# Sender attribute sums of a graph kernel: one-hots of 448 as the moving operand, attributes in two 12-bit parts

## The reference

```python
def _scatter_mean(vals, idx, num_segments):
    s = segment_sum(vals, idx, num_segments)
    cnt = segment_sum(ones(len(vals)), idx, num_segments)
    return s / maximum(cnt, 1.0)[:, None]
rec_attr  = _scatter_mean(edge_attr, row, N)     # row = src: the sender
sent_attr = _scatter_mean(edge_attr, col, N)     # col = dst: the receiver
out = concatenate([x, rec_attr, sent_attr], axis=1)
h = out @ W1 + b1;  h = where(h >= 0, h, 0.01 * h);  x + (h @ W2 + b2)
```

## Time and profile before

| what | value |
|---|---|
| median of 3 runs | 2954.69 us (2952.81 to 2959.83) |
| profiled execution | 2959.81 us, its span 2958.0 us |
| TensorE (PE) busy | 1953.7 us, 66% of the span |
| VectorE (DVE) busy | 1936.3 us, 65% |
| GpSimd (POOL) busy | 912.5 us, 31% |
| ScalarE (ACT) busy | 548.4 us, 19% |
| L1312, five matmuls of 425 columns x 83 | 312.7 us busy |
| L1328, 75 x 25 block matmuls | 293.9 + 147.7 us busy |
| L874, the products | 319.0 us busy |

### The profile page before, as it was taken

One profiled execution on the slowest core, in us unless ns is written; L12 is line 12 of the kernel. 1 busy time (PEld: TensorE's weight loads), 2 busy tenths in 40 slices (PEclk: granted clock), 3 DMA queues, 4 the chain that ended last, 5 costly groups with the idle time before them and its releaser, 6 DMA issues.

```text
span 2958.0 us, 37499 instructions
## 1 busy us (share of the span) xinstructions
PE 1953.7 (66%) x10211; PEld 1468.2 (50%) x10211; DVE 1936.3 (65%) x4804; ACT 548.4 (19%) x1179; POOL 912.5 (31%) x886
## 2 busy tenths in 40 slices
PE   3666679999999998535244334288745655656657
PEld 2211148877788886324233223277734444444446
DVE  8777777769877777646355436875575555556555
ACT  2444420000000001100000000022223333333332
POOL 2000000000000000276676677220025556556550
PEclk9666679999999999765555555588856667677778
DMA  5223244423443441334343343244211111111110
GB/s 172 116 123 133 113 156 175 171 82 129 156 178 106 172 173 63 113 103 114 103 131 105 107 114 106 68 117 125 85 41 41 41 40 43 42 43 43 40 42 27
DMA packets 98715, 299.72 MB, mean 101 GB/s; under 512 B 21472, under 2 KB 48871, under 8 KB 86240
## 3 DMA queue, kind: packets, MB, share of 16 engines
q1 hardware_dynamic: 69566, 232.90, 22.8%
q0 software_dynamic: 27712, 63.56, 8.2%
q10 hardware_dynamic: 1250, 0.86, 0.1%
HBM read 220.27 MB, written 76.97 MB: 100 GB/s over the span
## 4 chain that ended last, share of the span: by engine, by line
PE 41%; DVE 19%; POOL 14%; issue 13%; another core or an unknown queue 10%; DVEq 2%; ACT 1%; DMA 1%; ACTq 0%; SPq 0%; POOLq 0%
PE PS L1328 13%; PE PS L1312 8%; POOL G L520 8%; PE PS L1467 6%; PE PS L1432 5%; POOL SCR L520 5%; DVE SCR L848 3%; PE PS L1302 3%; DVE RX L1167 2%; DVE G L847 2%; DVE SCR L874 2%; PE PS L1455 2%; DVEq L1167 1%; DVE OH L836 1%
## 5 line engine op out<-in xcount | busy, mean ns | idle before, releaser
L520 POOL DMA_INDIRECT G<-table,src_idx x255 | 270.6, 1061 | 1271.8 <-DMA table<-RX 1164.4
L537 POOL DMA_INDIRECT G<-table,gather_idx x415 | 417.2, 1005 | 527.1 <-DMA table<-RX 247.6
L1387 PE MATMUL PS<-RX,OH 128*128 x830 | 224.0, 437 | 317.5 <-issue 247.8
L1167 DVE TENSOR_TENSOR RX<-RX,PS 128x256 f32 x415 | 173.0, 417 | 293.5 <-remote 241.1
L1387 PEld LDWEIGHTS PS<-RX,OH 128*128 128x128 f32 x830 | 185.6, 313 | 358.5 <-issue 356.3
L1467 PE MATMUL PS<-SCR,OH 128*128 128x256 f32 x830 | 281.0, 502 | 94.3 <-DVE SCR L1202 73.0
L874 DVE TENSOR_TENSOR SCR<-G,AT 128x2125 f32<-128x2125 f32 x83 | 319.0, 3843 | 0.0
L1312 PE MATMUL PS<-SCR,OH 128*128 128x425 f32 x830 | 312.7, 523 | 2.2 <-DVE G L882 1.8
L1328 PE MATMUL PS<-HB,RX 128*128 128x132 f32 (+1 forms) x2500 | 293.9, 278 | 1.0 <-ACT RX L590 1.0
L1302 PE MATMUL PS<-SCR,G 128*128 128x400 bf16 x590 | 212.4, 487 | 115.6 <-DVE SCR L848 53.0
L1328 PEld LDWEIGHTS PS<-HB,RX 128*128 128x128 f32 x2500 | 285.3, 192 | 1.5 <-ACT RX L590 1.5
(11 more groups left out here) (298 smaller groups left out, 2595.1 us busy)
## 6 DMA issues: line engine op xcount, KB each, us to landing
RX<-adjacency SPq DMA_DIRECT2D x66, 1600.0 KB, 6.7
adjacency<-RX SPq DMA_DIRECT2D x25, 1600.0 KB, 5.2
RX<-gathered_rows SPq DMA_DIRECT2D x83, 320.0 KB, 2.9
gathered_rows<-G SPq DMA_DIRECT2D x51, 320.0 KB
AT<-dst_in_block SPq DMA_DIRECT2D x83, 160.0 KB
gathered_rows<-SCR SPq DMA_DIRECT2D x32, 320.0 KB
G<-table,gather_idx POOLq DMA_INDIRECT x415
G<-table,src_idx POOLq DMA_INDIRECT x255
```

What stands on the lines that cost most here:

```text
L520: pool.indirect_dma_start(score_rows(i)[:, q], None, tables[0], bass.IndirectOffsetOnAxis(ap=src_idx[:, v:v + 1], axis=0)).then_inc(s(f"sc ...
L537: pool.indirect_dma_start(G[:, p, q, :], None, tables[i], bass.IndirectOffsetOnAxis(ap=gather_idx[:, p, q:q + 1], axis=0)).then_inc(s(f"{n ...
L1167: dve.tensor_tensor(acc, acc, PS[:, q, 0:MSG], ALU.add).then_inc(s("added"), 1)
L1387: ins = pe.matmul(view(PS, k % DEPTH * 1024 + 171 * q, [[1, XR_W]]), view(OH, (k % DEPTH * VB + q) * P, [[1, P]]), view(RX, b * XR_W, [[1, ...
```

## The change

The senders' sum is turned around. The 3125 nodes are cut into 7 groups of 448. The stationary operand holds 7 x 17 = 119 columns, the attributes times "is this the sender's group", and the moving one is a one-hot of 448, the sender's place in its group. Both are `float32r`, a second fp32 type of the tensor engine. The attributes are cut into two parts, the upper 20 bits of the word (sign, exponent, the leading bits of the mantissa) and the rest, so there are two matmuls for each visit, ten for each batch. The sums now lie as 119 rows (group, attribute) by 448 nodes, so the counts must be spread over 16 rows by one matmul and the means picked out by seven others. The batches lie in steps 0 to 62 (20 of these have two), and the means are made among steps 63 to 72 and not behind step 74.

```diff
+FULL = 63
+GRP = 7
+NSRC = 448
+LA = GRP * SA
+PARTS_L = 2
-            BATCH_OF.append([k, k + 1] if NBLK <= n < NBLK + NB - LAYERS * NBLK else [k])
+        BATCH_OF = [list(range(NB * n // FULL, NB * (n + 1) // FULL)) if n < FULL else [] for n in range(LAYERS * NBLK)]
 def attr_batch(k):                                            # VectorE
                 dve.tensor_copy(part(0), attrs(16))
-                split = mark(dve.tensor_tensor(sbh([[NBLK, VB], [1, NBLK]]), ..., ALU.is_equal))
-                one_hot(OHS(p), 2, k)
+                is_in()
+                split = mark(dve.tensor_scalar(half(HIGH_AT).bitcast(I32), attrs(SA).bitcast(I32), 12, 12, ALU.logical_shift_right,
+                                               ALU.logical_shift_left))
+                for q in range(VB):
+                    dve.tensor_scalar(hot_src(p, q), iota_h[:, 0:NSRC], view(EI, 2 * VW + VB * k + q, [[1, 1]]), None, ALU.is_equal)
                 dve.wait_ge(s("dve_step"), split)
-                dve.tensor_tensor(products(p), sbh([[NBLK, VB], [1, NBLK], [0, SA]]),
-                                  view(AT, VB * k, [[1, VB], [0, NBLK], [NV + 1, SA]]), ALU.mult)
+                dve.tensor_tensor(left, attrs(16), part(0), ALU.subtract)
+                split = mark(dve.tensor_tensor(half(LOW_AT), attrs(SA), half(HIGH_AT), ALU.subtract))
+                dve.tensor_tensor(into(0), member, by_group(HIGH_AT), ALU.mult)
                 dve.wait_ge(s("dve_step"), split)
                 split = mark(dve.tensor_copy(part(1), left))
+                dve.tensor_tensor(into(1), member, by_group(LOW_AT), ALU.mult)
+                dve.wait_ge(s("dve_step"), split)
+                split = mark(dve.tensor_tensor(left, left, part(1), ALU.subtract))
...
 def attr_sums(k):                                             # TensorE
                 for q in range(VB):
-                    pe.matmul(PS[:, 2, 0:NBLK * SA], OHS(p)[:, q], products(p)[:, q], start=False, stop=False, skip_group_check=True)
+                    for j in range(PARTS_L):
+                        pe.matmul(PS[0:LA, 2, 0:NSRC], grouped(p, j)[:, q * LA:(q + 1) * LA], hot_src(p, q),
+                                  start=False, stop=False, skip_group_check=True)
...
 VectorE, after update_block(n):
+                if n == FULL:
+                    attr_means()
+                if n == FULL + 2:
+                    dve.wait_ge(s("src_means_picked"), 1)
+                    src_sums = view(SUMS, 0, [[1, NSRC]], LA)
+                    dve.tensor_tensor(src_sums, src_sums, PS[0:LA, 2, 0:NSRC], ALU.mult).then_inc(s("means_ready"), 1)
...
 TensorE, after the batches of step n:
+                if n == FULL + 1:
+                    pe.wait_ge(s("means_ready"), 1)
+                    pe.matmul(PS[0:LA, 2, 0:NSRC], view(SUMS, 2 * NSRC, [[1, LA]], LA), view(SUMS, NSRC, [[1, NSRC]], LA), ...)
+                    pe.wait_ge(s("means_ready"), 2)
+                for g in range(7):
+                    if n == FULL + 1 + (g + 1) // 2:
+                        turn_means(g)
+                    if n == FULL + 6 + (g + 1) // 2:
+                        pick_means(g)
 setup, for each of four groups of visits:
-                dve.tensor_scalar(view(HT, 1536, [[1, P]]).bitcast(I32), idr[:, 0:P], 7, None, ALU.arith_shift_right)
-                dve.tensor_scalar(view(HT, 1664, [[1, P]]).bitcast(I32), idr[:, 0:P], 127, None, ALU.bitwise_and)
+                dve.tensor_scalar(sixteenth, idr[:, 0:P], 4, None, ALU.arith_shift_right)
-                dve.tensor_copy(st[2], view(HT, 1664, [[1, P]]).bitcast(I32))
-                dve.tensor_copy(vc, view(HT, 1536, [[1, P]]).bitcast(I32))
+                dve.tensor_scalar(group, sixteenth, 73.0, 36.0, ALU.mult, ALU.add)
+                dve.tensor_scalar(sixteenth, group, 11, None, ALU.arith_shift_right)
+                done(dve.tensor_copy(vc, sixteenth))
+                dve.tensor_scalar(st[2], vc, -float(NSRC), 1.0, ALU.mult, ALU.add)
+                dve.tensor_tensor(st[2], st[2], st[0], ALU.add)
```

More of the change, by code:

```diff
@@ L72 @@
 assert CB * CHUNKS == NBLK
+assert GRP * NSRC >= NODES and all((s * 73 + 36) >> 11 == s * SUBW // NSRC for s in range(SUBS))
 assert NB * VB == NV and (NB - PEEL) % DEPTH == 0 and 24 <= SLOT and AB * AV == NVA and SUBS % 2 == 0
@@ L104, in gnn_program @@
         HT = (RX, HT_AT)
+        with nc.sbuf_tensor("HOT_R", [P, 2 * VB * NSRC], F32R) as HOT_R:
+            pass
         SCR = sb("SCR", [P, 7680])
@@ L107, in gnn_program @@
         EI = sb("EI", [P, 5, VW])
+        with nc.sbuf_tensor("GROUPED_GAP", [P, DEPTH * VB * (D + P) - 4 * VB * LA - 4], F32):
+            with nc.sbuf_tensor("GROUPED_R", [P, 4 * VB * LA], F32R) as GROUPED_R:
+                pass
         G = sb("G", [P, DEPTH, VB, D])
@@ L119, in gnn_program @@
         iota = sb("iota", [P, P])
-        iota_h = sb("iota_h", [P, KEYS + P], mybir.dt.int16)
+        iota_h = sb("iota_h", [P, NSRC + P], mybir.dt.int16)
         zeros_b = sb("zeros_b", [P, KEYS], BF16)
@@ L867, in attr_batch @@
-                sbh = lambda dims: view(G, SBH_AT + p * VB * NBLK, dims)
+                left = view(G, LEFT_AT, [[16, VB], [1, 16]])
+                half = lambda at: view(G, at, [[SA, VB], [1, SA]])
+                by_group = lambda at: view(G, at, [[SA, VB], [0, GRP], [1, SA]])
+                into = lambda j: grouped(p, j).rearrange("p (v g a) -> p v g a", v=VB, g=GRP)
                 dve.tensor_copy(part(0), attrs(16))
-                split = mark(dve.tensor_tensor(sbh([[NBLK, VB], [1, NBLK]]), view(iota, 0, [[0, VB], [1, NBLK]]),
-                                               view(EI, VW + VB * k, [[1, VB], [0, NBLK]]), ALU.is_equal))
@@ L871, in attr_batch @@
-                one_hot(OHS(p), 2, k)
+                is_in()
[3 more added lines that the diff above has]
+                    dve.tensor_scalar(hot_src(p, q), iota_h[:, 0:NSRC], view(EI, 2 * VW + VB * k + q, [[1, 1]]), None, ALU.is_equal)
                 dve.wait_ge(s("dve_step"), split)
-                split = mark(dve.tensor_tensor(left, attrs(16), part(0), ALU.subtract))
@@ L1317, in attr_sums, with turn_means, pick_means @@
                 ins.then_inc(s("attrs_summed"), 1)
+            def turn_means(g):
+                w = min(4, NBLK - 4 * g)
+                if g >= 2:
+                    pe.wait_ge(s("mt_ready"), g - 1)
+                for b in range(w):
+                    ins = pe.transpose(PS[0:32, 4 + g % 2, b * P:(b + 1) * P], means[:, 4 * g + b, :], ident[:])
+                ins.then_inc(s("means_turned"), 1)
+            def pick_means(g):
+                if g == 0:
+                    pe.wait_ge(s("means_ready"), 3)
+                if g >= 2:
+                    pe.wait_ge(s("mt_ready"), 7 + g - 1)
+                pe.matmul(PS[0:16, 6 + g % 2, 0:NSRC], ident[0:LA, g * SA:g * SA + 16], view(SUMS, 0, [[1, NSRC]], LA),
+                          start=True, stop=True).then_inc(s("src_means_picked"), 1)
             pe.wait_ge(s("pair_copied"), SUBS // 2)
```

88 lines of the change are left out of this document (48 added, 40 removed).

## The result

The changed kernel takes 2857.8 us (median of 4 runs, 2853.9 to 2861.7) against 2957.3 us of the kernel before on the same chip (2952.8 to 2965.3): a ratio of 0.966 (95% interval 0.963 to 0.969), faster by 99 us. The forecast was 2832 us, with a range of 2800 to 2900. The profiled execution took 2858.4 us, its span 2856.6.

What follows compares the result with a forecast made beforehand. TensorE was taken to set the time of the 75 steps. Terms of -138 + 7.7 - 1 - 2.8 + 1.5 + 8.2 + 1.9 gave -122.5 us: 2837 from the profiled execution, 2832 from the median, range 2800 to 2900.

Steps and rivals of the forecast that it cites:

- TensorE's batches: Attribute matmuls of the 83 batches: 3.69 us a batch becomes 2.03, at one pass a matmul; 306 becomes 168 us, -138.
- stalls at steps 25 and 50: TensorE's waits at layer changes, 6.8 and 5.9 us, plus 4.4 for slow steps: 17.1 against 9.4 before, +7.7 us.
- start: Beginning of the 75 steps: batch 0 comes 1.2 us earlier, a gain of 1 us.
- eight doubles of before: The eight steps with two batches in the kernel before, bound by VectorE: -2.8 us.
- VectorE late in the first layer: Before the first layer change, where VectorE's margin is thin, a little lateness: +1.5 us.
- tail: Means moved among steps 64 to 72: 11.3 us more on TensorE, less 3.1 gained at the norm, +8.2 us.
- setup: VectorE's extra operations per group of 128 visits, +0.46 us for each of four groups: +1.9 us.
- the rivals of two and four passes: Attribute matmuls take two passes (2985 us, chance 0.03) or four (3298 us, chance 0.05), slower than before.
- The rival of loads that aren't hidden: Weight loads of the attribute matmuls stand open: +94 us, at most 2926 us; chance 0.06.
- limit of the first layer: VectorE's batch stays hidden up to 5.44 us in the first layer; forecast batch 5.26, 0.18 to spare.
- sign "near 1036": Sign in the trace: the norm behind the 75 steps begins near 1036 us instead of 1161.
- That the clock might fall: Clock falling in the shorter gaps, among other things 1 to 3% late; chance 0.05.

Runs made afterwards that it cites:

- true_fp32: The changed kernel with both operands of the attribute matmuls in plain fp32, all else the same: 3063.0 us, ratio 1.125 to the kernel before.
- columns: The changed kernel with 448, 352, 256 or 192 moving columns in the attribute matmuls, by batch in turn: 2571.6 us, one run.
- columns2: The changed kernel with 400, 320, 288 or 224 moving columns in the attribute matmuls, by batch in turn: 2566.0 us, one run.
- weights: The changed kernel with the stationary operand 119, 64, 32 or 128 columns wide, by batch in turn: 2611.8 us.
- one_part: The changed kernel with only the upper part multiplied on TensorE, five matmuls a batch, VectorE's work kept: 2563.5 us, ratio 0.941 to the kernel before.
- change_again: The changed kernel itself, unaltered, on the chips of the experiments: 2610.9 us against 2722.8 for the kernel before, ratio 0.959.
- single_at_rounds: The changed kernel with the second batch of steps 25 and 50 moved to the step behind: 2596.1 us, ratio 0.954 to the kernel before.

## Why the prediction was right

The mechanism was the one forecast; one term was too large by a tenth. That the type needs one pass was read from the diff and from no row, as the forecast says, so this much was a choice that held, with 0.08 put on two or four passes. By its own steps, to the start of the second norm:

| term | forecast | measured |
|---|---|---|
| TensorE's batches | -138 | -125 |
| stalls at steps 25 and 50 | +7.7 | +7.5 |
| start | -1 | -2.5 |
| eight doubles of before | -2.8 | -2.0 |
| VectorE late in the first layer | +1.5 | 0 |
| tail | +8.2 | +9.7 |
| setup | +1.9 | +1.8 |
| sum | -122.5 | -110 |

- **The batches, the step that was mis-sized.** 63 steps have a batch and 20 of them a second: 63 x 2.17 + 20 x 2.26 = 182 us, where 168 was forecast; before, a batch made a step longer by 9.41 - 5.71 = 3.70 us, 307 for the 83. The "one pass" was right: the rivals of two and four passes fall, and true_fp32 shows what four cost. The failed part is 0.714/4.03 x 448/425 = 0.187 us, which took the rate of an fp32 pass for this type. It is 0.203 (the change's trace), on a line of 0.45 ns a column (columns, columns2), and not by the load (weights). The rival of loads that aren't hidden falls too: a width of 32 costs what 128 does. By the figure for a load that the forecast gave from the Trainium skill (TensorE: Matmul & The Clock Gate, section LDWEIGHTS), loads in line would have made a matmul 0.099 us longer; the trace doesn't show it.
- **VectorE stayed hidden**, as the forecast had it from its rows: one-hots 446 ns each (0.44 forecast, from the row of 640), products 0.69 (0.69), the batch 5.31 (5.26). With the longer batches of TensorE the limit of the first layer is (3 x 7.88 + 2.26 - 3.45)/4 = 5.61 instead of 5.44, and the 1.5 us of lateness did not come: from step 1 on, the steps of the first layer with one batch take 7.88 us and those with two 10.13 to 10.15, up to the wait at step 25. That the margin was thin is shown by one_part. (The forecast's limit for the later layers, 5.9, is (3 x 5.67 + 4 x 2.03 - 1.8)/4 = 5.83 by its own numbers, which changes nothing here.)
- **The stalls.** 6.19 and 5.72 us for 6.8 and 5.9, slow steps 2.59 + 2.18 for 4.4: 16.7 us for 17.1; the stall before, in the same reading, was 7.21 + 2.01 = 9.2. In change_again the same sum is 15.0, and single_at_rounds took away nearly all of that and gained 14.8. That the forecast's 4.4 us for the slow steps came so near is in part luck, as the two profiles of the change have 4.8 and 3.1.
- **The start.** Step 1 begins 10.6 us after step 0 where it was 14.6, 2.7 and 5.2 us over a normal step with one batch: batch 0 is no longer waited for (it was 1.85 us), and it runs at full clock (1.00 in 417 to 421 us), where before its L1312 took 5.53 us in place of 3.74 (0.66 in 416 to 421 us). The block matmuls of step 0 still start at a low clock (0.63 in 409 to 417 us).
- **The doubles of before.** Steps 26 to 32 last 93.4 us, and seven times 5.67 + 2 x 3.70 are 91.5.
- **The tail.** The wait is 2.07 us (2.4 forecast), the reciprocal 2.95 us (3.2), the norm follows the update in 0.71. The 12 steps from 969.51 us take 13.0 us more than their block matmuls (11.3 forecast), which less the 3.97 - 0.71 gained at the norm is the 9.7. Of the 13.0, 1.6 are the low clock behind the wait, which the forecast had not charged and which is no certain cost (it came in four of nine profiles).
- **The setup.** Step 0 begins 1.8 us later and the first norm 2.3.
- **The rest.** -110 at the second norm becomes -101 in the profiled pair, as the last two stages were 9 us longer, and -112 on another chip, where they are equal. The forecast let them only move forward. Its miss of 26 us on the first chip is made up so: 12 to the second norm (13 of matmuls, while the smaller terms nearly cancel), 9 in stages that the change doesn't touch, and 4.5 because the median lies 0.6 us below the profiled execution where the forecast took off 5. Its sign "near 1036" for the norm doesn't fit its own sum, which gives 1161.5 - 122.5 = 1039; it was 1051.

That the clock might fall had a small chance in the forecast; it held at 0.98 and 0.99.

## What to carry to other kernels

Turning this product around pays nothing on TensorE by itself, 448 columns for 425 and twice the matmuls; there the type pays, and in fp32 the turned form with its two parts cost 340 us. Count passes x columns of both forms first, and ask what the other engine must build for each. Give the rate of a type that no row shows a margin (it was 8% off the nearest row). When a cut shortens the engine that bounds, write down the margin of the next engine in us a batch (0.3 us here), and look at the places where both meet without slack: two batches placed one step later were worth 15 us beside the stage's 112. A wait can cost more than its length, as the clock may fall behind it: 1.5 to 3.0 us more for a step behind each wait of 5.7 to 9.5 us in these profiles, and 1.3 to 1.6 more or nothing behind one of 2.07.

## What the hardware showed that was not expected

- The reduced fp32 type on TensorE: 3 ns + 0.45 ns a moving column (256 to 448 columns, with 119 stationary ones), 0.104 to 0.105 us at 192 and 224 columns, and 0.07 to 0.09 us more at the first matmul of a run. At 448 moving columns the width of the stationary operand, 32 to 128, does not change it. An fp32 pass over 448 columns takes 0.188 us, this one 0.203. The Trainium skill (FP8 and Floating Point Precision, section TensorE Precision Notes) tells of the passes and of a reduced mode, as the forecast said; the four passes agree with true_fp32 (0.751 us for 448 columns).
- VectorE writes this type as fast as fp32. A tensor_scalar from int16 takes 446 ns for 448 elements, and 447 into fp32 (true_fp32); the products of 595 elements take 769 ns into either.
- The granted clock after a wait of 2.07 us was 0.61 in the change's profile (984 to 988 us), and in others, after the same wait, the step behind ran at its normal 5.75 us: slow in four profiles of nine.
